# Attention and routed experts on one core: queries and keys transposed by DMA instead of TensorE and ScalarE

## The chip, the core and the metric

The kernel runs on one NeuronCore of a Trainium2 chip. The metric is the device time of one execution in microseconds (us). TensorE is PE in the profile, VectorE is DVE, ScalarE is ACT, GpSimd is POOL and SyncE is SP. Two queues carry nearly all DMAs: q1, whose DMAs SP issues, and q0, whose DMAs POOL issues.

## The reference

```python
# x: (2, 2048, 256); 4 heads of 64; 8 experts
x = x + ln(attention(ln(x)))
x = x + ln(moe(ln(x)))

def attention(x):
    xn = layernorm(x, ln_gamma, ln_beta)
    q, k, v = heads(xn @ w_q.T), heads(xn @ w_k.T), heads(xn @ w_v.T)
    qn = q / max(norm(q) * 64 ** -0.5, 1e-8) * q_gamma * 64 ** -0.5
    kn = k / max(norm(k) * 64 ** -0.5, 1e-8) * k_gamma
    return softmax(qn @ kn.T) @ v @ w_o.T + b_o          # heads put together again

def moe(x):
    e = argmax(x @ gate_w.T)
    return x + expert_w[e] @ x
```

Inputs and outputs are float32.

## The kernel before

The two batches are worked one after the other. For each there is a projection stage, a score stage and an output stage; the experts come behind both. In the projection stage 2048 tokens are taken as 16 tiles of 128 (`n` counts tiles over both batches, `t` is the tile in its group of four). TensorE projects a tile into two alternating PSUM banks (`ps_QK[t % 2]`, and another pair for the values). The rest of the tile's work is a line of small instructions, with an order written out by hand on each engine:

- ACT `squares` (L595 to L601): squares of queries and keys, the values' high half, and the gate copy. DVE `sums` (L964, L967): sums of the squares, and the values' low half.
- ACT `norms` (L618): the root. DVE `normal_qk` (L972, L975, L983): guard against zero, reciprocal, normalized queries and keys in float32.
- POOL (L459, L463): gamma on the queries, their squares. ACT `high_qk` (L626) and DVE `low_qk` (L992, L995): the float32 values are split into a high and a low float16 part, which lie beside each other in a row buffer `qk_s[t % 2]`, with tokens on partitions and 8 blocks (4 heads of queries, 4 of keys) of 128 columns.
- PE `transpose_qk` (L1461, L1463): eight 128x128 transposes into banks 6 and 7. ACT `move_q` and `move_k` (L632, L637) copy them into `q_T` and `k_T`; DVE's `move_q` (L1092) does the last two tiles' queries.
- SP `turned_keys` (L334, L335): after each group of four tiles, two DMAs copy the group's keys into the other plane of `k_T` with the 64-row halves swapped.

`high_qk` of tile n waits until the transposes of tile n-2 have read the same row buffer. On TensorE the order is projection of tile n+1, then transposes of tile n-1; the projection of n+1 waits for `normal_qk` of n-1, whose bank it takes. On ACT `high_qk` of n-1 stands between `squares` and `norms` of n.

Before the projection of batch 0, SP has put three large transfers on q1: the fill of `rows_d` (L324, 5,180 KB) and two of expert weights (L329, 512 KB each). Batch 1's stage has DVE's `page` work (routing) behind its first tile, and POOL issues one scatter for each tile (L434).

In the score stage, for each of 128 steps of a batch (4 heads, 2 blocks of 1024 queries, 16 tiles of keys), TensorE makes 128x1024 scores, ACT the exponentials (L695), a cast DMA that POOL issues (L482) the high half, DVE the low half (L1128), and TensorE 24 products with the values (L1618, L1619, L1620). The row buffers `qk_s` lie in the memory of the exponentials' float16 slots 2 and 3, so the first steps of the score stage wait for the last transposes. Group gi's keys are awaited before step 4 gi through `s_kc`.

## Time and profile before

| | us |
|---|---|
| median of 3 runs | 696.52 (695.33 to 700.66) |
| the profiled execution | 696.07 |
| its span in the trace | 694.3 |
| TensorE busy | 607.2 (87%) |
| VectorE busy | 579.8 (84%) |
| ScalarE busy | 536.5 (77%) |
| GpSimd busy | 262.9 (38%) |

By the timeline the projection stages run from about 25 to 82 us and from 312 to 382 us, the score stages from there to 275 and 570 us, and the rest is the output stages and the experts. A busy share is an average over these stages, which have different limits, so each stage is read by itself.

### The profile page before, as it was taken

What the parts mean: (1) busy time and instruction counts of PE and PEld (TensorE: products, weight loads), DVE (VectorE), ACT (ScalarE), POOL (GpSimd) and SP (SyncE); (2) the same over time, 40 slices, a digit from 0 to 9 for tenths busy, and PEclk for the clock granted to TensorE, in tenths of its full rate; (3) what the DMA queues carried; (4) which work ended last, traced back from release to release, by engine and by line L of the source; (5) the groups of instructions that cost most, each with busy time, mean ns of one, the idle gap of its engine ahead of it and who ended that gap; (6) DMA issues with size and microseconds to landing.
All of it is one profiled execution on the core that took longest, in us unless ns stands there. A gap on an engine that the chain in (4) does not pass through costs nothing.

```text
span 694.3 us, 21582 instructions
## 1 busy us (share of the span) xinstructions
PE 607.2 (87%) x8717; PEld 424.6 (61%) x8717; DVE 579.8 (84%) x1147; ACT 536.5 (77%) x876; POOL 262.9 (38%) x430
## 2 busy tenths in 40 slices
PE   4889789999999999877998899999999998658871
PEld 2667446666656667745766366666666677536761
DVE  5999868998898899898999588888988888977663
ACT  4688879888988899765897878888888897445552
POOL 4344433333333332002677433333323320455554
PEclk9999989999999999999999999999999999979997
DMA  5951198989889997122122888988898974119211
GB/s 165 290 130 31 33 182 163 171 156 184 166 157 168 170 172 149 64 62 68 47 85 69 159 155 156 165 156 162 155 166 151 165 135 124 55 69 314 72 58 47
DMA packets 60665, 92.88 MB, mean 134 GB/s; under 512 B 7057, under 2 KB 29844, under 8 KB 60566
## 3 DMA queue, kind: packets, MB, share of 16 engines
q0 software_dynamic: 35088, 66.13, 49.6%
q1 hardware_dynamic: 24902, 25.37, 12.8%
q8 instruction: 69, 1.13, 0.7%
q14 instruction: 30, 0.25, 0.1%
q10 hardware_dynamic: 576, 0.00, 0.0%
HBM read 15.87 MB, written 14.66 MB: 44 GB/s over the span
## 4 chain that ended last, share of the span: by engine, by line
PE 50%; DVE 25%; ACT 9%; issue 7%; DMA 5%; POOL 1%; another core or an unknown queue 1%; SPq 0%; POOLq 0%; DVEq 0%; ACTq 0%
PE banks L1576 18%; PE banks L1619 7%; PE banks L1618 7%; PE banks L1620 7%; PE banks L1370 5%; DVE e_l L1128 4%; DMA e_h<-e_f 2%; ACT e_f L695 2%; DVE x_all L1201 2%; PE banks L1420 2%; DMA e_x<-x_all 2%; ACT x_all L695 2%; DVE st L1214 1%; DVE e_l L983 1%; PE banks L1468 1%
## 5 line engine op out<-in xcount | busy, mean ns | idle before, releaser
L695 ACT ACTIVATE e_f<-banks,nbias,c_ 128x1024 f32<-128x1024 f32 x172 | 200.6, 1202 | 43.2 <-PE banks L1576 31.4
L1576 PE MATMUL banks<-q_T,k_T 128*128 128x512 f16 (+1 forms) x1024 | 217.2, 384 | 9.1 <-DVE e_l L983 3.9
L1620 PE MATMUL banks<-v_mm,e_l 128*128 128x65 f16 x2048 | 203.4, 192 | 0.0
L1620 PEld LDWEIGHTS banks<-v_mm,e_l 128*128 128x128 f16 x2048 | 187.9, 98 | 0.0
L1128 DVE TENSOR_TENSOR e_l<-e_f,e_h 128x1024 f16<-128x1024 f32 x100 | 120.1, 1224 | 20.4 <-DMA e_h<-e_f 13.5
L1618 PE MATMUL banks<-v_mm,e_h 128*128 128x65 f16 x1184 | 118.9, 193 | 1.2 <-issue 0.6
L1619 PE MATMUL banks<-v_mm,e_h 128*128 128x64 f16 x1184 | 119.1, 194 | 0.0
L1618 PEld LDWEIGHTS banks<-v_mm,e_h 128*128 128x128 f16 x1184 | 108.9, 97 | 13.6 <-issue 2.2
L1619 PEld LDWEIGHTS banks<-v_mm,e_h 128*128 128x128 f16 x1184 | 108.5, 97 | 9.8
L1576 PEld LDWEIGHTS banks<-q_T,k_T 128*128 128x128 f16 (+1 forms) x1024 | 51.3, 96 | 99.6 <-issue 62.1
L695 ACT ACTIVATE x_all<-banks,nbias,c_ 128x1024 f32<-128x1024 f32 x84 | 98.9, 1201 | 6.9 <-DVE e_l L1128 5.5
L1128 DVE TENSOR_TENSOR e_l<-e_f,e_x 128x1024 f16<-128x1024 f32 x72 | 86.5, 1223 | 10.5 <-DMA e_x<-e_f 6.2
L1619 PE MATMUL banks<-v_mm,e_x 128*128 128x64 f16 x864 | 87.2, 194 | 0.0
L1618 PE MATMUL banks<-v_mm,e_x 128*128 128x65 f16 x864 | 87.2, 193 | 0.0
L1618 PEld LDWEIGHTS banks<-v_mm,e_x 128*128 128x128 f16 x864 | 79.4, 97 | 11.3 <-issue 4.0
L482 POOL DMA_DIRECT2D e_h<-e_f x86 | 46.1, 536 | 101.9 <-PE banks L1620 66.0
L1619 PEld LDWEIGHTS banks<-v_mm,e_x 128*128 128x128 f16 x864 | 79.2, 97 | 6.9
L482 POOL DMA_DIRECT2D e_x<-e_f x62 | 33.1, 534 | 80.9 <-PE banks L1620 62.4
L1128 DVE TENSOR_TENSOR e_l<-x_all,e_h 128x1024 f16<-128x1024 f32 x48 | 57.9, 1225 | 2.2 <-DMA e_h<-x_all 1.4
L459 POOL TENSOR_TENSOR e_l<-e_l,gq 128x256 f32<-128x256 f32 x32 | 33.8, 1055 | 67.2 <-DVE e_l L983 66.8
L1128 DVE TENSOR_TENSOR e_l<-x_all,e_x 128x1024 f16<-128x1024 f32 x36 | 43.7, 1221 | 6.2 <-DMA e_x<-x_all 6.0
L434 POOL DMA_INDIRECT rows_d<-attn_x,rowat x32 | 32.1, 1002 | 31.1 <-DVE rowat L1295 18.6
(304 smaller groups left out, 1257.1 us busy)
## 6 DMA issues: line engine op xcount, KB each, us to landing
e_h<-e_f POOLq DMA_DIRECT2D x86, 256.0 KB, 3.8
e_x<-e_f POOLq DMA_DIRECT2D x62, 256.0 KB, 3.7
e_h<-x_all POOLq DMA_DIRECT2D x42, 256.0 KB, 4.1
e_x<-x_all POOLq DMA_DIRECT2D x30, 256.0 KB, 4.6
x_all<-x SPq DMA_DIRECT2D x12, 512.0 KB, 4.2
rows_d<-e_x SPq DMA_DIRECT2D x1, 5180.0 KB, 25.5
k_T<-k_T SPq DMA_DIRECT2D x16, 256.0 KB, 3.6
k_T<-rows_d SPq DMA_DIRECT2D x15, 259.0 KB, 5.5
```

What stands on the lines that cost most here:

```text
L434: pool.indirect_dma_start(out=rows_d, out_offset=bass.IndirectOffsetOnAxis(ap=rowat[:, b * NT + i:b * NT + i + 1], axis=0), in_=x1_all[:, ...
L459: pool.tensor_tensor(qv, qv, spread(gq[:, :], 1, H), ALU.mult).then_inc(s_qg, 1)
L482: pool.dma_start(high[s % ALL % NHI], whole[s % ALL % NEF]).then_inc(s_cast[s % ALL % NHI], 16)
L695: act.activation(whole[s % ALL % NEF], ps_S[s % ALL % 3], ACT.Exp, bias=bias_of(h, k // NT), scale=CESC).then_inc(s_E, 1)
L1128: dve.tensor_tensor(low[s % ALL % NLO], whole[s % ALL % NEF], high[s % ALL % NHI], ALU.subtract).then_inc(s_El, 1)
L1201: dve.scalar_tensor_tensor(out=x_all[:, 2 * i + t, :], in0=ps_Y[i][t][:, 0:D], scalar=rs1[:, i % 2, t:t + 1], in1=x_all[:, 2 * i + t, :], ...
L1370: ins = pe.matmul(dst, l, r, start=(i == 0), stop=(i == n - 1))
L1420: pe.matmul(ps_QK[t % 2], l, r, start=i == 0, stop=False)
L1576: return pe.matmul(ps_S[s % ALL % 3][:, c * BANK:(c + 1) * BANK], k_T[rows, 1 - c if cross else c, h * N + j * P:h * N + (j + 1) * P], q_T ...
L1618: pe.matmul(o, high[s % ALL % NHI][:, at], v[:, 0:DH + 1], start=first, stop=False, skip_group_check=True)
L1619: pe.matmul(o[:, 0:DH], high[s % ALL % NHI][:, at], v[:, VL:VS], start=False, stop=False, skip_group_check=True)
L1620: ins = pe.matmul(o, low[s % ALL % NLO][:, at], v[:, 0:DH + 1], start=False, stop=j == NT - 1, skip_group_check=True)
```

## The change

Three edits. First, the eight transposes and two copies of a tile are replaced by two transposing DMAs on SP's queue, one for the queries (128x512 float16 in, four blocks of 128x128 out) and one for the keys. They count on `s_tr[n % 2]`, 32 a tile. What waited for the transposes (`high_qk`, POOL's and DVE's first steps of the score stage, TensorE's first scores, the keys' swap) now waits for these DMAs to land. Second, the guard of the norm (L972) is merged into the multiplication that follows: `min(1/norm, limit) * value` is one scalar_tensor_tensor, and the scale of the keys moves into constants. Third, the values' low halves leave the buffer `v_mm`, where they began at a byte that isn't a multiple of 8 in half of the cases, and get a tile `v_lo` of their own; the rows of `v_mm` become 68 elements long.

```diff
-        v_mm = sb("v_mm", [P, NT * H, VS], f16)       # VS = 130
+        v_mm = sb("v_mm", [P, NT * H, VS], f16)       # VS = 68
+        v_lo = sb("v_lo", [P, NT * H, DH], f16)
...
+            def transposed_qk(n, at):
+                sp.wait_ge(s_lo, n + 1)
+                if n == 0:
+                    sp.wait_ge(s_wf, 2)
+                for i, plane in ((0, 0), (1, 1 + swapped(at))):
+                    sp.dma_start_transpose(qk_T[:, plane, :].rearrange("p (h n) -> p h n", h=H)[:, :, at * P:(at + 1) * P],
+                                           qk_rows[n % 2][:, i * H * P:(i + 1) * H * P]).then_inc(s_tr[n % 2], 16)
+
+            def turned_keys(b, gi):
+                a = swapped(gi * TG)
+                for i in range(2):
+                    sp.wait_ge(s_tr[i], transposed(b * NT + (gi + 1) * TG - 2 + i))
...
+            def queries_and_keys(b):
+                for at in range(NT):
+                    transposed_qk(b * NT + at, at)
+                    if at % TG == 0 and at:
+                        turned_keys(b, at // TG - 1)
+                turned_keys(b, NG - 1)
...
                     if s == b * ALL + 2:
-                        pool.wait_ge(s_T2, b * NT + NT - 1)
+                        pool.wait_ge(s_tr[0], transposed(b * NT + NT - 2))
...
                 def high_qk(n, t):
...
                     if n - 1 > 0:
-                        act.wait_ge(s_T2, n - 1)
+                        act.wait_ge(s_tr[t % 2], transposed(n - 2))
...
-                        if not (first and t < 2):
-                            move_k(n - 2, at - 2)
-                            move_q(n - 2, at - 2)
...
                         if h == 0 and k == 0:
                             high_qk(end - 1, NT - 1)
-                            move_k(end - 2, NT - 2)
-                        if h == 0 and k == 1:
-                            move_k(end - 1, NT - 1)
...
-                    dve.scalar_tensor_tensor(out=nm[:, :], in0=nr[:, :], scalar=RMS_EPS, in1=rcol[:, :],
-                                             op0=ALU.max, op1=ALU.mult).then_inc(s_dq, 1)
-                    dve.wait_ge(s_dq, 2 * n + 1)
-                    dve.reciprocal(rn[:, :], nm[:, :]).then_inc(s_dq, 1)
+                    dve.reciprocal(rn[:, :], nr[:, :]).then_inc(s_dq, 1)
...
-                    dve.tensor_tensor(qk_n[t % 2].rearrange("p (h d) -> p h d", d=DH),
-                                      ps_QK[t % 2].rearrange("p (h d) -> p h d", d=DH),
-                                      spread(rn[:, :], 2, DH), ALU.mult).then_inc(s_qkn, 1)
+                    dve.scalar_tensor_tensor(out=qk_n[t % 2].rearrange("p (h d) -> p h d", d=DH), in0=spread(rn[:, :], 2, DH),
+                                             scalar=KSCALE / RMS_EPS, in1=ps_QK[t % 2].rearrange("p (h d) -> p h d", d=DH),
+                                             op0=ALU.min, op1=ALU.mult).then_inc(s_qkn, 1)
...
                     if s == b * ALL + 2:
-                        dve.wait_ge(s_T2, end)
+                        dve.wait_ge(s_tr[1], transposed(end - 1))
...
-                        if not (first and t < 1) and not (last and t == TG - 1):
-                            transpose_qk(n - 1, t - 1)
...
-                        pe.matmul(o[:, 0:DH], high[s % ALL % NHI][:, at], v[:, VL:VS], start=False, stop=False, skip_group_check=True)
+                        pe.matmul(o[:, 0:DH], high[s % ALL % NHI][:, at], v_l, start=False, stop=False, skip_group_check=True)
```

## Rows read from the trace of the kernel before

**Rows 1.** The page's first line: the span.
```profile
span 694.3 us, 21582 instructions
```

**Rows 2.** Busy times by stretch: PE, PEld, DVE, ACT, POOL, granted clock, DMA share, GB/s.
```profile
322.65:333.36 10.71, 8.18 (x45) 5.54 (x43) 10.26 (x35) 4.02 (x10) 5.57 (x6) 0.84 0.07 25
333.36:349.00 15.64, 13.63 (x99) 10.68 (x97) 14.11 (x40) 13.91 (x35) 9.76 (x11) 1.00 0.24 69
349.00:363.30 14.30, 13.27 (x96) 10.60 (x96) 13.07 (x31) 13.29 (x33) 10.48 (x13) 1.00 0.25 72
363.30:377.70 14.40, 13.33 (x94) 10.19 (x92) 13.00 (x32) 11.31 (x30) 10.35 (x12) 1.00 0.25 74
```

**Rows 3.** Timeline of two tiles: start us, us, engine, line, operation, idle before it.
```profile
366.68 0.68 DVE L992 TENSOR_TENSOR e_h<-e_l,e_h 128x512 f16<-128x512 f32 x1
...
368.21 0.69 DVE L964 TENSOR_REDUCE ss<-e_f 128x8 f32<-128x512 f32 x1 [0.41 <-ACT e_f L595]
...
369.35 0.17 DVE L972 SCALAR_TENSOR_TENSOR nm<-nr,rcol 128x8 f32<-128x8 f32 x1
...
371.14 0.40 PE L1461 MATMUL banks<-ident,e_l 128*128 128x128 f16 x4 [0.46 <-DVE e_l L992]
...
371.57 0.71 PE L1420 MATMUL banks<-wqkv_h,n_h 128*128 128x512 f32 x2
...
371.70 0.63 ACT L626 ACTIVATE e_h<-e_l 128x512 f16<-128x512 f32 x1
```

**Rows 4.** Groups by line and shape, 349.0 to 377.7 us: busy, mean ns, idle before.
```profile
L964 DVE TENSOR_REDUCE ss<-e_f 128x8 f32<-128x512 f32 x8 | 5.4, 681 | 1.7 <-ACT e_f L595 1.7
L972 DVE SCALAR_TENSOR_TENSOR nm<-nr,rcol 128x8 f32<-128x8 f32 x8 | 1.3, 164 | 0.3
...
L632 ACT ACTIVATE q_T<-banks 128x512 f16<-128x512 f16 x8 | 4.9, 614 | 0.0
L637 ACT ACTIVATE k_T<-banks 128x512 f16<-128x512 f16 x8 | 4.8, 603 | 0.0
```

**Rows 5.** The swap of the keys, the two issuing lines L334 and L335.
```profile
L334 SPq DMA_DIRECT2D k_T<-k_T x8: 590/591/716, 44.4 to 387.4; - x8
...
DMA to landing us min/median/max: 3.2/3.3/3.4
...
L335 SPq DMA_DIRECT2D k_T<-k_T x8: 608/624/640, 45.2 to 388.0; - x8
...
DMA to landing us min/median/max: 3.7/4.1/4.4
```

**Rows 6.** The page's table of queues: packets, MB, share of 16 engines' span.
```profile
q1 hardware_dynamic: 24902, 25.37, 12.8%
```

**Rows 7.** Start of batch 0: weights' issues, landing, DMA share, ACT.
```profile
L329 SPq DMA_DIRECT2D x_all<-weT x2: 483/4776/9070, 21.3 to 30.4; - x2
...
DMA to landing us min/median/max: 12.8/16.6/20.4
...
42.00:44.00 2.00, 1.39 (x12) 1.26 (x13) 2.00 (x5) 2.00 (x7) 1.72 (x2) 1.00 0.08 33
...
35.52 0.64 ACT L626 ACTIVATE e_h<-e_l 128x512 f16<-128x512 f32 x1
```

**Rows 8.** Timeline where batch 1's projection ends and its scores begin.
```profile
386.73 0.60 ACT L637 ACTIVATE k_T<-banks 128x512 f16<-128x512 f16 x1 [0.70 <-PE banks L1463]
...
387.23 2.30 ACT L695 ACTIVATE e_f<-banks,nbias,c_ 128x1024 f32<-128x1024 f32 x2
...
389.27 0.53 POOL L482 DMA_DIRECT2D e_h<-e_f  x1 [2.38 <-ACT e_f L695]
```

**Rows 9.** Timeline of the products with the values, head 0 and head 3.
```profile
390.24 0.19 PE L1618 MATMUL banks<-v_mm,e_h 128*128 128x65 f16 x1 [0.30 <-issue]
...
390.87 0.19 PE L1618 MATMUL banks<-v_mm,e_h 128*128 128x65 f16 x1
...
540.31 0.19 PE L1618 MATMUL banks<-v_mm,e_h 128*128 128x65 f16 x1
...
540.93 0.19 PE L1618 MATMUL banks<-v_mm,e_h 128*128 128x65 f16 x1
```

More of the change, by code:

```diff
@@ L227, in build @@
         s_kc = [sem(f"s_kc{i}") for i in range(NG)]
+        s_tr = [sem(f"s_tr{i}") for i in range(2)]
         s_id, s_ones, s_wf, s_qg, s_q2 = sems("id ones wf qg q2")
@@ L379, in _ @@
             pool.memset(ones16[:, :], 1.0).then_inc(s_ones, 1)
-            for i in range(2 * H):
-                pool.memset(rcol[:, i:i + 1], 1.0 if i < H else 1.0 / KSCALE).then_inc(s_ones, 1)
             pool.memset(v_mm[:, :, DH:DH + 1], 1.0).then_inc(s_ones, 1)
@@ L1449, in project_first_two @@
                 bias_v(1)
-            def transpose_qk(n, t):
-                qs = qk_s[t % 2]
-                pe.wait_ge(s_lo, n + 1)
-                if (sum(pb < b for pb, _, _ in PASSES) - 1) * PAGE + 2 > 0:
-                    pe.wait_ge(s_pg, (sum(pb < b for pb, _, _ in PASSES) - 1) * PAGE + 2)
-                if n > 0:
-                    pe.wait_ge(s_qe, n)
-                if n > 0:
-                    pe.wait_ge(s_ke, n)
-                for h in range(H):
-                    pe.transpose(ps_TQ[:, h * P:(h + 1) * P], qs[:, h, :], ident16[:, :])
-                for h in range(H):
-                    ins = pe.transpose(ps_TK[:, h * P:(h + 1) * P], qs[:, H + h, :], ident16[:, :])
-                ins.then_inc(s_T2, 1)
             def keep_running(count):
@@ L1609, in pv @@
                     pe.wait_ge(s_El, s + 1)
-                    v = v_mm[:, j * H + h, :]
+                    v, v_l = v_mm[:, j * H + h, :], v_lo[:, j * H + h, :]
                     for q in range(QT):
@@ L1657, in _ @@
                 hh = b * H
-                pe.wait_ge(s_ke, end - 3)
-                pe.wait_ge(s_qe, end - 3)
+                pe.wait_ge(s_tr[0], transposed(b * NT + QT - 2))
+                pe.wait_ge(s_tr[1], transposed(b * NT + QT - 1))
                 pe.wait_ge(s_mx, b + 1)
@@ L1663, in _ @@
                 scores(hh, 0, 1)
-                transpose_qk(end - 2, NT - 2)
                 pe.wait_ge(s_vl, end)
@@ L1673, in _ @@
                 largest_everywhere(1)
-                pe.wait_ge(s_ke, end)
                 pe.wait_ge(s_root, 9 * b + 1)
```

70 lines of the change are left out of this document (22 added, 48 removed).

## The prediction

> **What bounds the kernel now.** I read the page first: a span of 694.3 us [rows 1] in an execution of 696.07 us, so 1.8 us lie around the span, and the execution is 0.45 us under the median of the runs (696.52). My sum is made against 696.07. The busy shares cover stages with different limits, so I went on to the busy times by stretch. In the score stages TensorE sets the pace, and the change touches only the operands of its products with the values. In the projection stages three engines are nearly full at once: over tiles 8 to 15 of batch 1 (28.7 us, 3.59 us a tile) PE, DVE and ACT are busy 26.6, 26.1 and 24.6 us [rows 2]. The four tiles before, which also carry DVE's statistics for a later group, take 3.91 us each with DVE busy 14.11 of 15.64 us. So no engine is alone the bound, and the chain alternates between them. The groups by line say what DVE waits for: 1.7 of its 2.6 idle us are for ACT's squares [rows 4], which wait for a projection, which waits behind the transposes, which wait for `low_qk` (0.46 us in [rows 3]). That is the ring which the change cuts.
>
> **What is taken away.** Per tile, PE loses 8 transposes, 0.43 us from the first to the next projection (371.14 to 371.57, [rows 3]). ACT loses two copies, 0.61 + 0.60 us [rows 4]. DVE loses L972, 0.16 us, with the gap to the next about 0.21. PE's and ACT's savings count only as far as they shorten DVE's waits. So with free transposes tiles 8 to 15 lose 1.7 us of waits and 8 x 0.21 = 1.7: 28.7 becomes 25.3, or 3.16 us a tile, and DVE is then the bound. Tiles 4 to 7 lose 4 x 0.21 = 0.8. In batch 1 the projection behind the page work no longer waits for the first transposes: 0.6. At the end of the stage ACT no longer waits 0.70 us for the last transposes and copies them before the third exponential (386.73, then 387.23, [rows 8]), and an earlier copy goes too: 1.5. Together 3.4 + 0.8 + 1.5 = 5.7 us in batch 0 and 6.3 in batch 1, 12.0 in all. That is the most that the change can give.
>
> **Edits I cost at nothing.** L983 becomes a scalar_tensor_tensor over the same 512 float32 elements; no row has that form at that size. Bounds are 0 and 0.05 us a tile (1.6 us in all); I take 0. The values' alignment: the rows of `v_mm` are 260 bytes apart, so with the head number both halves pass through every offset of 4 bytes in 16. Head 0 makes 21 products from 390.24 to 390.87 and head 3 makes 21 from 540.31 to 540.93 [rows 9]: 0.63 and 0.62 us, one pace at opposite alignments. Nothing is gained there.
>
> **What is added: two DMAs a tile, with a round trip in a ring.** `high_qk` of tile n now waits until both DMAs of tile n-2 have landed. Call D the time from the end of `low_qk` to that landing. In the trace L992 ends at 367.36 and `high_qk` of the tile two further starts at 371.70 [rows 3]: 4.34 us, while two tiles last 7.1. `norms`, behind it on ACT, could come about 0.3 us later before DVE misses it. So D may be 2p - 2.5 at a pace of p a tile, or p = (D + 2.5) / 2. A late `high_qk` holds `norms`, then `normal_qk`, then the next projection: everything. At 3.59 us a tile D may be 4.7 us; for the best pace of 3.16 it must be under 3.8.
>
> What is D? The trace has no transposing DMA. The nearest row is the swap of the keys on the same queue [rows 5]: 0.59 us to issue, 3.2 to 3.4 us from issue to landing for the first and 3.7 to 4.4 for the second right behind it. It moves 256 KB in 256 pieces of 1 KB. If a transposing DMA costs no more, D = 0.1 + 0.59 + 3.3 to 4.1 = 4.0 to 4.8, the lower bound in practice. But a transposing DMA has no pieces of 1 KB: each row of the input holds four blocks of 128 columns, 256 bytes each, that go to different places, so it has at least 128 x 4 = 512 pieces. The queue's row gives 16 x 694.3 us x 0.128 / 24,902 = 57 ns a packet of about 1 KB on one engine [rows 6]. The swap's 16 pieces an engine take 0.9 of its 3.3 us, which leaves 2.4 that are fixed. The transposing DMA's 32 pieces an engine take 1.8 us at the price of a packet and 0.5 at the price of the bytes. The upper bound is pieces of a quarter of that size at the same price, 7.3 us a DMA. I take the price of a packet with pieces of 256 bytes, the middle case and the one nearest to the row: D = 0.1 + 2.4 + 2 x 1.8 = 6.1 us, p = 4.3.
>
> Then tiles 8 to 15 cost (4.33 - 3.59) x 8 = 5.9 us more, tiles 4 to 7 (4.33 - 3.91) x 4 = 1.7, the two before them about 0.8, and the swaps of the keys, which now stand between transposes on SP (2 x 0.6 us of issue) and put 0.9 us of packets each ahead of them, about 0.5 in each of three groups, 1.5. That is 9.9 us a batch, 19.8. The end of the stage still gains, but the third cast now waits for tile 14's DMAs instead of ACT, so I count 1.0 of the 1.5 in each batch: -2.0; and -0.6 behind the page work. The keys' last group is needed only at step 12, and hidden.
>
> The Trainium skill (VectorE: DVE Perf Modes, "The three transpose paths") puts a 128x128 transpose of 2-byte elements at 1309 ns by DMA against 390 ns on TensorE. No row here shows it; it speaks against the change. Taken one after the other, eight blocks would be an estimated 10.5 us a tile, and the whole near 890 us.
>
> **A stall at the start of batch 0.** SP's queue is not empty there. The second weights' issue starts at 30.4 us and lands 12.8 us later, at 43.2, and the DMA share falls to 0.08 only from 42 on [rows 7]. Tile 0's transposes are issued at about 31.3, behind those bytes, and can't land before them. `high_qk` of tile 2 ran at 35.52 [rows 7] and would wait to 43.2: 7.7 us, with DVE, ACT and PE all behind it. The bounds are 0, if the transposes pass the weights, and about 9, if TensorE's clock drops in the pause as it did to 0.84 around a similar one [rows 2].
>
> Sum: 19.8 - 2.0 - 0.6 + 7.7 = +24.9, and 696.1 + 24.9 = 721.
>
> **The rivals.**
> - *The round trip fits.* D = 4.3, p = 3.4. Tiles 8 to 15 gain 1.5 a batch, with 0.8 and 1.5 as above: 3.8 a batch and 0.6, 8.2 in all, against the stall of 7.7: 695.6, about no change. For it: the swap of the keys lands in 3.3 us with twice the bytes. Against: its pieces are four times larger. Chance 0.33, from 690 to 699. The Trainium skill (Advanced Engine Details and Errata, "X-Bar Transpose (TRN2)") says that transposing DMAs are as fast as regular ones; that is this rival, and by the page its 695.6 us would be the time.
> - *Faster.* The transposes are not held behind the weights at 31 us, and D is under 3.8, so DVE bounds at 3.16 us a tile: 696.1 - 12.0 = 684. It decides at one place, the stall: without its 7.7 us even the case above gives 688. Against: one queue, and 9.07 us for an issue in front of it that found the queue full [rows 7]. Chance 0.09.
> - *Much slower.* The pieces are 64 bytes or cost more than a packet: 7.3 us a DMA and 14.6 a tile, and the pace is that of the engines. 28 tiles x (14.6 - 3.7) = +305, about 1000 us at the bound; anything over 770 belongs here. Chance 0.13.
> - *The transposes don't matter*, because POOL's scatters and gamma (10.4 of 14.3 us busy in batch 1, [rows 2]) take over as the bound: then batch 1 gains nothing and batch 0's gain pays half of its stall, about 700. It is inside the first rival's sign and I give it 0.03.
>
> **How the numbers follow.** The forecast case has 0.42, from 703 (D = 5) to 770 (D = 8.5 to 9, or SP's issue twice as long). Together with the case that fits, the range is 690 to 770; under it lies 0.09 and over it 0.13. The likeliest case's own range is 703 to 770. About 1% is what a measurement of this kernel can tell from no change. Faster by over 1% (under 689.5) has 0.09, within 1% 0.36, slower 0.55. The predicted time is 721 us.
>
> **What would show it.** The landing of the two new DMAs on SP: I expect 5.5 to 6.5 us from `low_qk` to the second landing, and about 12 us for the first tile of batch 0, behind the weights. ACT's `high_qk` should show idle time ended by a DMA in most tiles; if its releaser is POOL as before, D fits. The starts of L964 should be 4.3 us apart in tiles 8 to 15; 3.2 to 3.4 would say that the ring fits, over 6 that the DMA engines or SP's issue bound. The issue of a transposing DMA should take 0.6 to 0.8 us; if it takes 2, SP is the bound and the forecast is low. Between 35 and 43 us all three engines should pause. L1618 should keep 30 ns from one product to the next. The prediction falls if the new DMAs land within 4 us, if tile 2 doesn't wait for the weights, or if packets of the new DMAs cost other than 57 ns.

## The result

| | median us | runs | ratio to before |
|---|---|---|---|
| before | 698.55 | 4 | |
| after | 708.23 (707.02 to 711.74) | 4 | 1.0166, 95% interval 1.0127 to 1.0205 |

The changed kernel is slower by 1.7%. (The kernel before has one run more here, 700.57 us, than the three behind the median of 696.52.) The profiled execution took 707.02 us, with a span of 705.3 us against 694.3 [rows 1]: +11.0 us, where the forecast had +24.9. The direction was right; the size was more than twice too large.

The page of the kernel after: the span, the engines' busy time, the granted clock in 40 slices, SP's queue (packets, MB, share of 16 engines' span) and the chain that ended last.

```profile
span 705.3 us, 20987 instructions
...
PE 601.7 (85%) x8461; PEld 416.7 (59%) x8461; DVE 572.2 (81%) x1111; ACT 509.1 (72%) x816; POOL 261.0 (37%) x422
...
PEclk9959979999999999999999899999999999879996
...
q1 hardware_dynamic: 59718, 33.77, 19.4%
...
PE 49%; DVE 23%; DMA 8%; issue 6%; ACT 6%; SPq 5%; POOL 1%; POOLq 0%; another core or an unknown queue 0%; ACTq 0%; DVEq 0%
```

SP's queue carries 59,718 packets instead of 24,902 [rows 6]. The 64 transposing DMAs account for the 34,816 more, 544 each. The line of the chain now has 8% of DMA and 5% of SP's queue, where the kernel before had 5% and 0%. The busy times by stretch (PE, PEld, DVE, ACT, POOL, granted clock, DMA share, GB/s) follow. The stretches are those of [rows 2], each moved by 11.02 us, because batch 1's tile 0 starts that much later:

```profile
333.67:344.38 10.71, 6.77 (x37) 4.31 (x36) 10.28 (x33) 4.15 (x12) 5.95 (x7) 1.00 0.25 61
344.38:360.02 15.64, 12.74 (x64) 9.64 (x62) 13.43 (x33) 10.09 (x26) 10.19 (x12) 0.89 0.41 99
360.02:374.32 14.30, 11.37 (x64) 8.85 (x64) 11.99 (x28) 10.17 (x25) 10.27 (x12) 1.00 0.64 150
374.32:388.72 14.40, 12.97 (x61) 9.55 (x61) 11.11 (x26) 6.79 (x19) 9.81 (x11) 0.88 0.67 122
```

In the third stretch PE and ACT are emptier than before (11.4 and 10.2 us against 13.3 and 13.3), and DVE, which was to become the bound, waits too (12.0 against 13.1). In the fourth DVE has 11.1 us against 13.0, and the granted clock, 1.00 before, is 0.88.

**Where the time went.** The last product of each tile's projection (the bias of the values, L1418; L1432 before) marks the tiles. These are its rows in the timeline of TensorE for tiles 0, 4, 5 and 15 of batch 0 and tiles 0 and 15 of batch 1, by start and duration:

```profile
19.84 0.28 PE L1418 MATMUL banks<-bq,ones 128*128 128x264 bf16 x1
...
36.44 0.44 PE L1418 MATMUL banks<-bq,ones 128*128 128x264 bf16 x1
...
49.92 0.44 PE L1418 MATMUL banks<-bq,ones 128*128 128x264 bf16 x1
...
88.18 0.29 PE L1418 MATMUL banks<-bq,ones 128*128 128x264 bf16 x1
...
325.99 0.29 PE L1418 MATMUL banks<-bq,ones 128*128 128x264 bf16 x1
...
388.18 0.29 PE L1418 MATMUL banks<-bq,ones 128*128 128x264 bf16 x1
```

From such rows, and for the last two columns from the last product of the scores, the stages of every kernel follow. All later uses of "stages" mean this table (us, in profiled executions; the labels are those of the experiments below):

| kernel | to tile 0 | projection, batch 0 | scores and output, batch 0 | projection, batch 1 | scores, batch 1 | rest | span |
|---|---|---|---|---|---|---|---|
| before | 20.9 | 57.6 | 236.5 | 62.5 | 191.5 | 125.4 | 694.3 |
| after | 19.8 | 68.3 | 237.8 | 62.2 | 192.1 | 125.0 | 705.3 |
| e1 merge only | 20.8 | 55.0 | 235.3 | 60.8 | 190.9 | 125.7 | 688.4 |
| e10 the same again | 21.6 | 55.0 | 235.5 | 59.8 | 190.4 | 125.6 | 687.8 |
| e2 clear start | 21.3 | 64.0 | 237.4 | 63.3 | 194.0 | 126.9 | 706.9 |
| e3 plain copies | 21.6 | 65.3 | 235.2 | 60.6 | 190.4 | 123.8 | 696.9 |
| e4 one DMA | 20.8 | 69.1 | 238.5 | 61.4 | 192.5 | 127.6 | 709.9 |
| e11 boundary order | 20.8 | 66.6 | 238.1 | 64.1 | 192.1 | 129.4 | 711.2 |
| e12 third DMA | 21.5 | 74.8 | 243.6 | 72.1 | 201.3 | 129.2 | 742.5 |
| e9 queries from tile 5 | 21.6 | 54.5 | 237.0 | 59.8 | 191.4 | 126.4 | 690.7 |
| e5 late fill * | 20.4 | 59.4 | 248.2 | 62.1 | 192.9 | 114.9 | 697.9 |
| e6 fillers * | 21.8 | 65.4 | 236.2 | 63.6 | 193.9 | 115.3 | 696.1 |
| e7 queries by DMA * | 21.5 | 65.1 | 234.6 | 59.0 | 192.0 | 114.5 | 686.8 |
| e8 merge, late fill * | 21.7 | 55.0 | 244.5 | 59.7 | 191.2 | 113.6 | 685.6 |

The four kernels with a star ran on another chip, where the last stage is 10 to 12 us shorter and the kernel before took 685.98 us. They are read by their other stages and by ratios to before on that chip.

The first two rows hold the result: +10.7 us in batch 0's projection, +1.3 behind it, and nothing else that counts. Batch 1's projection, for which the forecast had +9.3 (9.9 - 0.6; its gain of 1.0 at the end of the stage lies behind tile 15 and so in the next column), came out 0.3 us shorter. 13.5 us of batch 0 lie between two tiles, 36.44 to 49.92. ACT shows why. These are its rows for `high_qk` (L640) of tile 2, and of tile 9 in batch 1, with the idle time before and its releaser:

```profile
43.68 0.63 ACT L640 ACTIVATE e_h<-e_l 128x512 f16<-128x512 f32 x1 [11.63 <-DMA qk_T<-e_h]
...
371.40 0.63 ACT L640 ACTIVATE e_l<-e_l 128x512 f16<-128x512 f32 x1 [1.10 <-DMA qk_T<-e_l]
```

and SP's timeline around both (start, duration of the issue, count of instructions that the row merges):

```profile
31.49 7.13 SPq L336 DMA_TRANSPOSE qk_T<-e_h  x2
38.66 3.78 SPq L336 DMA_TRANSPOSE qk_T<-e_l  x2
...
366.97 2.50 SPq L336 DMA_TRANSPOSE qk_T<-e_l  x2
369.91 2.50 SPq L336 DMA_TRANSPOSE qk_T<-e_h  x2
372.51 0.60 SPq L343 DMA_DIRECT2D qk_T<-qk_T  x1
373.15 0.62 SPq L344 DMA_DIRECT2D qk_T<-qk_T  x1
373.82 3.15 SPq L336 DMA_TRANSPOSE qk_T<-e_l  x2
```

Tile 0's transposes are issued at 31.49 and release ACT at 43.68, 12.2 us later, where the prediction had "about 12". In the steady state a pair is issued in 2.50 us and has released ACT 4.4 us after the issue began (366.97 to 371.40). That is the first surprise: over half of the 4.4 us is the issue. All 64 together, the source view of L336 (min/median/max of the issue in ns):

```profile
L336 SPq DMA_TRANSPOSE qk_T<-e_h x32: 1188/1267/3837, 31.5 to 394.8; - x32
L336 SPq DMA_TRANSPOSE qk_T<-e_l x32: 1188/1268/2417, 38.7 to 398.4; - x32
```

The 1.3 us behind batch 0's projection go with a wait for DMAs too. The row buffers lie in memory that the first steps of the score stage need, so DVE's low half of the third step waits for the transposes of the last tile:

```profile
106.22 1.23 DVE L1114 TENSOR_TENSOR e_l<-e_f,e_h 128x1024 f16<-128x1024 f32 x1 [3.67 <-DMA qk_T<-e_l]
```

It starts 18.0 us behind tile 15's last product, where the kernel before had 15.6, and the sixth low half 24.5 us behind it, where the kernel before had 23.4.

**The last group boundary.** By the same rows the distances inside the groups of batch 1 are 3.2 us a tile for tiles 8 to 11 (362.75 to 372.23 in three steps) and 3.0 for tiles 12 to 15, against 3.6 and 3.4 before: the 3.16 of "free transposes" is there between the boundaries. But tile 12 stands 7.0 us behind tile 11 (4.0 before). TensorE's row there:

```profile
375.21 0.83 PE L1406 MATMUL banks<-wqkv_h,n_h 128*128 128x512 f32 x2 [2.69 <-DVE n_l L956]
```

and the stretches around it:

```profile
368.00:372.00 4.00, 4.00 (x29) 3.43 (x28) 3.06 (x7) 2.04 (x7) 3.56 (x5) 1.00 0.59 132
372.00:375.00 3.00, 0.51 (x5) 0.27 (x3) 2.80 (x5) 2.37 (x7) 2.06 (x3) 1.00 0.72 168
375.00:379.50 4.50, 4.29 (x15) 3.30 (x16) 2.98 (x8) 0.53 (x2) 3.21 (x4) 0.62 1.10 163
```

ACT waits 1.10 us for the transposes of tile 7, the tile two ahead in the same row buffer (371.40 above). Behind that on ACT stand the root of the norms and the high half of the next group's rows, and behind those on DVE stands their low half `n_l` (L956). TensorE idles 2.69 us for it, and for the next 4.5 us its granted clock is 0.62, near the lower of its two levels (1.2 of 2.4 GHz).

### The profile page after: what moved, and what is told of

It reads as the page before. It is cut to its first block, busy times and chain, and to the rows that moved or that the text cites. A ratio compares the mean times of both kernels' runs of the same rounds, so it can differ in the third digit from the quotient of the medians.

```text
span 705.3 us, 20987 instructions
## 1 busy us (share of the span) xinstructions
PE 601.7 (85%) x8461; PEld 416.7 (59%) x8461; DVE 572.2 (81%) x1111; ACT 509.1 (72%) x816; POOL 261.0 (37%) x422
## 3 DMA queue, kind: packets, MB, share of 16 engines
q1 hardware_dynamic: 59718, 33.77, 19.4%
## 4 chain that ended last, share of the span: by engine, by line
PE 49%; DVE 23%; DMA 8%; issue 6%; ACT 6%; SPq 5%; POOL 1%; POOLq 0%; another core or an unknown queue 0%; ACTq 0%; DVEq 0%
PE banks L1543 19%; PE banks L1585 7%; PE banks L1587 7%; PE banks L1586 7%; DMA qk_T<-e_l 4%; DVE e_l L1114 4%; SPq L336 4%; PE banks L1356 3%; ACT e_f L694 2%; DVE x_all L1187 2%; PE banks L1406 2%; DVE st L1200 2%; DVE e_l L976 1%; DMA qk_T<-e_h 1%; ACT x_all L694 1%
## 5 line engine op out<-in xcount | busy, mean ns | idle before, releaser
L1543 PE MATMUL banks<-qk_T 128*128 128x512 f16 (+1 forms) x1024 | 220.8, 388 | 12.3 <-DVE e_l L976 7.6
L1114 DVE TENSOR_TENSOR e_l<-e_f,e_h 128x1024 f16<-128x1024 f32 x100 | 120.8, 1226 | 22.4 <-DMA e_h<-e_f 10.7
L1585 PE MATMUL banks<-v_mm,e_h 128*128 128x65 f16 x1184 | 119.0, 195 | 3.9 <-DVE e_l L1114 2.8
L1586 PE MATMUL banks<-v_lo,e_h 128*128 128x64 f16 x1184 | 119.0, 193 | 0.0
L1585 PEld LDWEIGHTS banks<-v_mm,e_h 128*128 128x128 f16 x1184 | 108.6, 98 | 16.4 <-DVE e_l L1114 3.9
L1543 PEld LDWEIGHTS banks<-qk_T 128*128 128x128 f16 (+1 forms) x1024 | 51.8, 97 | 107.3 <-issue 66.7
L1586 PEld LDWEIGHTS banks<-v_lo,e_h 128*128 128x128 f16 x1184 | 108.1, 99 | 9.7
L1585 PE MATMUL banks<-v_mm,e_x 128*128 128x65 f16 x864 | 86.4, 194 | 0.0
L1586 PE MATMUL banks<-v_lo,e_x 128*128 128x64 f16 x864 | 86.3, 192 | 0.0
L1585 PEld LDWEIGHTS banks<-v_mm,e_x 128*128 128x128 f16 x864 | 78.7, 97 | 11.3 <-issue 2.5
L1586 PEld LDWEIGHTS banks<-v_lo,e_x 128*128 128x128 f16 x864 | 78.4, 98 | 6.9
L496 POOL DMA_DIRECT2D e_x<-e_f x62 | 33.1, 534 | 86.1 <-PE banks L1587 63.3
L448 POOL DMA_INDIRECT rows_d<-attn_x,rowat x32 | 32.0, 1000 | 31.6 <-DVE rowat L1281 20.8
## 6 DMA issues: line engine op xcount, KB each, us to landing
rows_d<-e_x SPq DMA_DIRECT2D x1, 5180.0 KB, 24.9
```

Source lines behind the costliest of these rows:

```text
L448: pool.indirect_dma_start(out=rows_d, out_offset=bass.IndirectOffsetOnAxis(ap=rowat[:, b * NT + i:b * NT + i + 1], axis=0), in_=x1_all[:, ...
L496: pool.dma_start(high[s % ALL % NHI], whole[s % ALL % NEF]).then_inc(s_cast[s % ALL % NHI], 16)
L1114: dve.tensor_tensor(low[s % ALL % NLO], whole[s % ALL % NEF], high[s % ALL % NHI], ALU.subtract).then_inc(s_El, 1)
L1543: return pe.matmul(ps_S[s % ALL % 3][:, c * BANK:(c + 1) * BANK], k_T[rows, 1 - c if cross else c, h * N + j * P:h * N + (j + 1) * P], q_T ...
L1585: pe.matmul(o, high[s % ALL % NHI][:, at], v[:, 0:DH + 1], start=first, stop=False, skip_group_check=True)
L1586: pe.matmul(o[:, 0:DH], high[s % ALL % NHI][:, at], v_l, start=False, stop=False, skip_group_check=True)
```

## The experiments

My theory after the result had three parts: the merged guard is a gain of its own; the ring of DMAs costs a little in every group; and the start of batch 0 costs a lot once. The rivals: the merge gives nothing, the start is a matter of the queue's order, and the boundary's idle time and clock are what costs. The edits are shown shortened.

**e1: the merge and the alignment alone.** The change without its DMAs; transposes stay on TensorE.

```diff
-  nr = sqrt(ss / DH);  nm = max(nr, eps) * rcol;  rn = 1 / nm;  qk_n = ps_QK * rn
+  nr = sqrt(ss / (DH * KSCALE**2));  rn = 1 / nr;  qk_n = min(rn, KSCALE / RMS_EPS) * ps_QK
+  v_lo = sb("v_lo", [P, NT * H, DH], f16)
```

> The kernel before with only the merged norm guard and the values' low halves in a tile of their own; the transposes stay on TensorE. If both edits matter only by the instruction they take from VectorE, each of 32 tiles loses about 0.2 us of which a part is hidden: 2 to 5 us faster than before (ratio 0.993 to 0.997), and the products with the values keep 30 ns. The rival, that the alignment of the low halves sets the pace of the products, would give 0.5 ns or more on each of 6144 products, 3 us on top, and a shorter spacing of L1618's successor.

Measured: 690.51 us against 697.04, ratio 0.9919 (0.9890 to 0.9949). Stages: batch 0's projection 55.0 us (57.6 before), batch 1's 60.8 (62.5), the others within 1.2 us of before. So the two small edits give 4.3 us in the projections, and 6.5 us in the whole, a little over the 2 to 5 expected. It is the guard: DVE's low half of the values takes 473 ns in both kernels, aligned or not. Set against this kernel, the DMAs cost 13.3 us in batch 0's projection and 1.4 to 2.4 in batch 1's.

**e10: the same again, on a third chip**, beside e9, e11 and e12.

> The kernel before with the merged guard and the aligned low halves alone, transposes on TensorE, once more and on the same chip as the other three, so that they can be set against it: 0.992 of before again (0.989 to 0.995 the first time), if the ratios carry over from chip to chip.

Measured: 694.30 against 698.83, ratio 0.9932 (0.9907 to 0.9957). The gain is real and carries over. The profiled execution was the fastest of six (689.49 us), so its span, 687.8, flatters this kernel.

**e2: a clear start.** The changed kernel with the fill of `rows_d` on POOL's queue, and the experts' first weights issued behind tile 8.

```diff
-  sp.dma_start(rows_d..., absent...)                       # before the transposes
+  pool.dma_start(rows_d..., absent...)
-  for k in range(KH): sp.dma_start(raw_we[:, k], ...)      # before the transposes
+  if b == 0 and at == 8: for k in range(KH): sp.dma_start(raw_we[:, k], ...)
```

> The changed kernel, with the 5,180 KB fill issued on GpSimd's queue and the first expert weights issued behind the transposes of tile 8, so that SP's queue is empty when the first transposes are issued. If the changed kernel loses its time at that one place (ScalarE's wait of 11.6 us for the first transposes of the row buffer e_h), it becomes 8 to 11 us faster than the changed kernel: 697 to 700 us, no change against before. If the round trip of every tile sets the pace, the wait moves to the later tiles and less than 3 us come back: 705 or more.

Measured: 710.37, ratio 1.0222 (1.0176 to 1.0269). ACT's row for tile 2, the stretches of the start, and the source view of the fill:

```profile
40.65 0.63 ACT L642 ACTIVATE e_h<-e_l 128x512 f16<-128x512 f32 x1 [7.18 <-DMA qk_T<-e_h]
```

```profile
18.00:28.00 10.00, 9.95 (x66) 8.05 (x65) 9.32 (x28) 6.76 (x21) 4.04 (x7) 1.00 1.04 302
28.00:38.00 10.00, 6.52 (x28) 4.77 (x27) 7.54 (x21) 3.95 (x10) 2.33 (x3) 0.76 1.07 258
```

```profile
L423 POOL DMA_DIRECT2D rows_d<-e_x x1: 2233/2233/2233, 14.3 to 14.3; - x1
...
DMA to landing us min/median/max: 25.4/25.4/25.4
```

Nothing stands ahead of the transposes on SP's queue any more, and ACT still waits 7.2 us. What is left is the fill on the other queue, issued at 14.3 us and landed at 39.7, with the DMA share over 1 from 18 to 38 us (1.04, 1.07). The trace has the single DMA packets too: the first one of the transposes starts at 35.36, 5.1 us behind the issue at 30.23, where it is 1.2 us in the steady state. So the order of one queue explains only part of the wait; transfers of the other queue hold the transposes back too. The prediction had blamed the weights in front of them on SP. Batch 0's projection is 4.3 us shorter than in the changed kernel, but the kernel isn't: the other stages are about 6 us longer together. DVE's waits for the last tiles' transposes (5.9 us against 3.7) are a part of that; for the rest I have no cause.

**e5 and e8: the fill behind batch 0's scores.** e5 is the changed kernel, e8 that of e1. In both POOL issues the fill when the score stage of batch 0 ends; in e5 the weights are behind tile 8 as well.

```diff
+  if b == 0:
+      pool.wait_ge(s_PV, ALL)
+      pool.memset(absent, NTOK);  pool.dma_start(rows_d..., absent...)
```

> The changed kernel with the 5,180 KB fill moved behind batch 0's score stage (issued by GpSimd, from the same memory) and the first weights behind tile 8's transposes. In the run that only changed the queue of the fill, ScalarE still waited 7.2 us for the first transposes, with the DMA engines at a share of 1.0 to 1.1 until 39.7 us, when the fill landed. Theory: the DMA engines, not the queue, hold the first transposes. Then, with the engines free, ScalarE's first wait for a DMA in batch 0 falls under 1 us, tile 15's projection starts 7 to 9 us sooner than in the changed kernel (79 to 81 us instead of 88), and the time becomes 699 to 703 us, unless the fill gives 1 to 3 us back in the output stage. Rival: the first transposing DMAs are slow by themselves (the first issue in the trace took 3.8 us); then a wait over 4 us stays, and the time stays over 705.

> The kernel before with the merged guard, the values' own tile and the late fill, all transposes on TensorE. It is the control of the late fill alone: in batch 0's projection stage nothing waits for a DMA, so the late fill should give nothing there, and at most 2 us either way in the output stage: 689 to 693 us against 690.5. If it is 3 us or more faster, the fill held something in the first 40 us in the kernel before too, and that part of the gain of the changed kernel with the late fill is not the transposes'.

Measured: e5 699.43 against 685.98, ratio 1.0208 (1.0185 to 1.0230); e8 686.81, ratio 1.0006 (0.9991 to 1.0020). e5's row for tile 2:

```profile
33.45 0.63 ACT L645 ACTIVATE e_h<-e_l 128x512 f16<-128x512 f32 x1 [0.86 <-DMA qk_T<-e_h]
```

The wait falls from 11.63 to 0.86 us and batch 0's projection from 68.3 to 59.4: the stall of the start is the DMA engines' load, and it is worth 8.9 us. (The two kernels ran on different chips; e1 and e8, on the same two, both have 55.0 us in this stage.) But the fill costs 10.4 us where it now stands (248.2 against 237.8), and 9.2 in e8 (244.5 against 235.3), so moving it wins nothing. The two kernels also give the price of the DMA way with no stall at the start. e5's projections are 4.4 and 2.4 us longer than e8's, and its span is 12.3 us longer. Of the other 5.4 us of stages, 3.7 lie in the scores and output of batch 0, 1.7 in batch 1's scores and 1.3 in the rest, less 1.3 before tile 0. In both score stages DVE's third low half waits for the last tile's transposes, 4.11 and 2.70 us, and the sixth comes 1.6 and 0.8 us later than in e8; for the remainder I have no cause.

**e3: plain copies.** The two transposing DMAs are replaced by plain copies of the same bytes from and to the same places. Queries and keys are then not transposed, and the factor of the exponent is set to 0, so this kernel leaves out the transposition and its scores mean nothing; tokens may be routed otherwise, and its last stage isn't compared.

```diff
-  sp.dma_start_transpose(qk_T[:, plane]..., qk_rows[n % 2][...])
+  sp.dma_start(qk_T[:, plane]..., qk_rows[n % 2][...].rearrange("p (h n) -> p h n", h=H))
-  dve.tensor_scalar(CESC, tmp[3], 1.0 / (KSCALE * sqrt(DH)), ...)
+  dve.tensor_scalar(CESC, tmp[3], 0.0, ...)
```

> The changed kernel with each transposing DMA replaced by a plain DMA over the same bytes and blocks (so queries and keys aren't transposed; the factor of the exponent is set to zero to keep the numbers finite). It prices the transposing itself. If a transposing DMA costs more than a copy by its issue on SP (1.2 us against about 0.6) and its landing, the copies land about 1.3 us sooner, ScalarE's waits for DMAs fall from 25 us to under 10 us outside the first tile, and the time falls by 2 to 5 us. If the landing is set by the number of 256-byte pieces, the same for both, the time stays within 1 us of the changed kernel.

Measured: 700.39 against 697.04, ratio 1.0054 (1.0028 to 1.0079). The source view of the copies:

```profile
L336 SPq DMA_DIRECT2D qk_T<-e_h x32: 593/641/3052, 32.8 to 388.1; - x32
L336 SPq DMA_DIRECT2D qk_T<-e_l x32: 594/641/4221, 36.7 to 390.7; - x32
...
  ACT e_h L640: 11.9, 1
  ACT e_l L640: 1.9, 2
```

A copy's issue takes 0.64 us, half a transposing DMA's. With it ACT waits for these DMAs three times in all instead of 15: once 11.9 us at the start, where copies are held back like transposes, and 1.9 us in two others. Batch 1's projection is 60.6 us, as with the merge alone. So away from the start a pair of copies is hidden, and what the ring notices is what a pair of transposing DMAs costs beyond it. That is the issue, 2.50 us a pair instead of 1.28. By the DMA packets in the two traces, a pair in batch 1 that nothing disturbs has its last packet 3.9 us behind the start of its issue as transposes and 2.6 us as copies, but 1.4 us behind the end of its issue as either.

**e4: one DMA of eight blocks** in place of two of four, in the two groups where queries and keys lie side by side.

```diff
-  for i, plane in ((0, 0), (1, 1)): sp.dma_start_transpose(qk_T[:, plane]..., ...)
+  sp.dma_start_transpose(qk_T[:, 0:2]..., qk_rows[n % 2])      # 128x1024 in, 8 blocks out
```

> The changed kernel with one transposing DMA of eight blocks instead of two of four in the first and third group of each batch, two as before in the second and fourth. If the issue of a transposing DMA costs by the block (a piece at a time from SP), the single one takes about 2.4 us on SP, as the two together do, and nothing changes. If it costs by the instruction, it takes about 1.25 us, the pair of groups shows a landing 1.2 us sooner, and 2 to 4 us are gained.

Measured: 711.65 us, one execution. SP's timeline, where L337 is the pair of four-block DMAs and L340 the single one of eight blocks:

```profile
370.37 2.50 SPq L337 DMA_TRANSPOSE qk_T<-e_l  x2
373.41 1.23 SPq L340 DMA_TRANSPOSE qk_T<-e_h  x1
```

Eight blocks are issued in 1.23 us, like four: the issue goes by the instruction. Yet the projections are no shorter (69.1 and 61.4 us against 68.3 and 62.2). By the packets the single DMA is done 2.6 us behind the start of its issue, where the pair takes 3.9: the round trip is shorter by the issue that is saved. Yet halving the issue in half of the groups didn't show in the whole, in this one execution.

**e6: fillers at the boundary.** Eight products without use ahead of TensorE's wait at each boundary.

```diff
   if t == TG - 1:
+      if g: keep_running(8)
       pe.wait_ge(s_ys, g + 2)
```

> The changed kernel with 8 products that nobody reads (about 1.8 us) on TensorE before the first projection of each group but the second. In the changed kernel TensorE is idle for 2.7 us there and the projection then runs at the granted clock of 1.2 GHz: 4.0 us instead of 2.6. Theory: the transposes on TensorE also kept its clock up, and their removal costs about 1.4 us at each boundary. Then with the products the projections behind the boundaries take 2.6 us again, and 3 to 6 us come back (702 to 705 us). Rival: the pace is that of the DMAs' round trip and the slow projections are hidden by it: the time stays within 1.5 us of the changed kernel's.

Measured: 698.59 against 685.98, ratio 1.0196 (1.0179 to 1.0213). TensorE's row at the boundary and the stretch from it:

```profile
374.46 0.73 PE L1406 MATMUL banks<-wqkv_h,n_h 128*128 128x512 f32 x2 [2.61 <-DVE n_l L956]
```

```profile
374.00:377.00 3.00, 2.54 (x9) 1.76 (x10) 2.97 (x7) 0.40 (x2) 1.92 (x3) 0.76 0.81 177
```

The fillers were done at 371.85, and TensorE still idled 2.61 us; the clock still fell, and over the 4.5 us from the restart it is 0.62, as in the changed kernel (375.21 to 379.71). The experiment doesn't separate idle time from clock, and is inconclusive on that; e11 does.

**e7: queries alone by DMA,** keys on TensorE and ScalarE, with the merge.

```diff
-  for h in range(H): pe.transpose(ps_TQ[:, h * P:(h + 1) * P], qs[:, h, :], ident16)   # and move_q on ACT
+  sp.dma_start_transpose(q_T[...][:, :, at * P:(at + 1) * P], qk_rows[n % 2][:, 0:H * P])
```

> The kernel before with the merged guard and the values' own tile, and only the queries transposed by DMA (one a tile); the keys stay on TensorE and ScalarE. By the theory that the round trip of two DMAs (2.5 us of issue and about 2 us to land) is what costs, one of them costs half of the issue, 1.25 us, and lands 3.2 us after the low half is written, inside the 4.3 us that the ring leaves; only the start of batch 0 still waits for the fill. So it lies between: 4 to 8 us slower than the 690.5 us of the same kernel without DMAs (694 to 699). If the number of DMAs doesn't matter and the boundaries and the start cost the same, it is as slow as the changed kernel, 706 or more.

Measured: 689.71 against 685.98, ratio 1.0063 (1.0044 to 1.0083). ACT's row for tile 2:

```profile
44.76 0.63 ACT L643 ACTIVATE e_h<-e_l 128x512 f16<-128x512 f32 x1 [10.11 <-DMA q_T<-e_h]
```

Half of the DMAs leave the start as bad as all (65.1 us for batch 0's projection). Batch 1's is 59.0 us, 0.7 under e8's on the same chip. Away from the start, one transposing DMA a tile is hidden; two are not. The ratio of 1.0063 is above what had been expected (at most 699 us, 1.003), because the stall at the start stayed whole.

**e9: queries by DMA from tile 5 of batch 0 on.** As e7, but tiles 0 to 4 take the old way, so that nothing is transposed by DMA while the fill and the weights are under way.

```diff
+  FD = 5
+  if b * NT + at >= FD: transposed_q(b * NT + at, at)     # on SP
-  move_q(n - 2, at - 2)
+  if n - 2 < FD: move_q(n - 2, at - 2)                    # on ACT
```

> The kernel before with the merged guard and the aligned low halves; keys stay on TensorE and ScalarE, and queries go by one transposing DMA a tile, but only from tile 5 of batch 0 on: tiles 0 to 4 take the old way, so nothing waits for a transposing DMA while the fill of the rows and the weights hold the DMA engines. Theory A (the loss of the DMA way is the start of batch 0 and the wait at the last group boundary, both of which this leaves out; elsewhere one DMA a tile that is issued in 1.25 us and has landed within about 4.4 us is hidden): batch 0's projection about 54 us (55.0 with the merge alone), batch 1's about 59 to 60 (60.8), ScalarE's casts of the high halves wait for no DMA, and the kernel is 1 to 2 us below the merge alone: ratio to before about 0.990. Theory B (each transposing DMA costs time wherever it stands, as SP's queue, the keys' swap or the shared write port is held by it): batch 0's projection 56 us or more, ratio 0.995 or more, above the merge alone.

Measured: 692.65 against 698.83, ratio 0.9919 (0.9893 to 0.9946), beside e10's 694.30 and 0.9932. Batch 0's projection takes 54.5 us, and ACT's waits in both projections name no DMA: the start is avoided as theory A had it. Batch 1's is 59.8, no shorter than e10's. The two versions can't be told apart: the intervals overlap, and by spans e9 is the longer (690.7 against 687.8), but e10's is that of its fastest execution. Both are faster than the two kernels of this case.

**e11: another order at the boundary.** In the third tile of a group, ACT takes the norms' root and the next group's high half ahead of `high_qk`, and DVE the low half ahead of `low_qk`.

```diff
+  if t == 2: norms(n);  high_y(g + 1)
   high_qk(n - 1, t - 1)
-  norms(n) ... if t == 2 and not last: high_y(g + 1)
+  if t != 2: norms(n)
```

> The changed kernel with another order in the third tile of each group alone: ScalarE takes the tile's root and the high half of the next group's rows ahead of the cast that waits for the transposing DMA, and VectorE the low half of those rows ahead of the low half of the queries and keys. Theory A (at a boundary the wait for the transposes of two tiles ago, 1.10 us at 371.40, is passed on through this order to the next group's rows, TensorE idles 2.7 us and comes back at half clock): the start distance over the last boundary falls from 7.0 and 8.1 us to about 4.5, the granted clock there stays at full, each batch's projection is 2 to 4 us shorter (about 65 and 59 to 60 us), and the ratio falls from 1.017 to about 1.009. Theory B (the boundary is late for another reason, such as the group's rows themselves or TensorE's clock): distances stay at 7 and 8 us and the ratio at 1.015 to 1.02.

Measured: 712.02 against 698.83, ratio 1.0169 (1.0135 to 1.0203), that of the change itself. TensorE's row at the boundary, then its stretch, then SP and ACT behind it:

```profile
374.19 0.73 PE L1409 MATMUL banks<-wqkv_h,n_h 128*128 128x512 f32 x2 [0.43 <-DVE n_l L959]
```

```profile
374.00:377.00 3.00, 2.81 (x15) 2.10 (x15) 2.97 (x8) 1.67 (x6) 1.61 (x2) 1.00 0.77 185
```

```profile
374.76 2.51 SPq L336 DMA_TRANSPOSE qk_T<-e_l  x2
...
380.97 0.63 ACT L640 ACTIVATE e_l<-e_l 128x512 f16<-128x512 f32 x1 [2.88 <-DMA qk_T<-e_l]
```

This was the most useful experiment. At the boundary everything happened as theory A said: TensorE idles 0.43 us instead of 2.69, the granted clock stays at 1.00, and tile 12 starts 3.2 us behind tile 11 (7.0 in the kernel after; 3.5 for 8.1 in batch 0). And nothing was gained, where that theory had about 0.8%: 2.88 us of waiting appear in the next round, for the transposes that were issued at 374.76, just behind the swap of the keys. The wait at the boundary was where the ring's debt was paid, not its cause. It also takes the clock out of the account: at 1.00 instead of 0.62 the kernel was no faster.

**e12: a third transposing DMA a tile,** the keys once more into the half that the swap overwrites.

```diff
-  for i, plane in ((0, 0), (1, 1 + swapped(at))):
+  for i, plane in ((0, 0), (1, 1 + swapped(at)), (1, 2 - swapped(at))):
```

> The changed kernel with a third transposing DMA a tile: the keys once more, into the half that the swap of the keys overwrites later, so that the results are the same. Theory A (the time of a transposing DMA is its issue, 1.25 us on SP, and its packets, 544 of about 22 ns each: the third adds at least 1.25 us to the time D from low halves to landed, and the two-buffer ring gives a pace of (D + 2.5)/2, but SP needs 3.75 us a tile and so sets it): the pace inside the groups of batch 1 rises from 3.2 us to 3.8 to 4.2, batch 1's projection from 62 us to 70 to 76, batch 0's by as much, and the ratio is 1.04 to 1.06. Theory B (the ring has room, what costs is only the start and the boundary): pace stays at 3.2 to 3.4 us, ratio below 1.03.

Measured: 742.42 against 698.83, ratio 1.0634 (1.0584 to 1.0683), a little over theory A's range. The source view:

```profile
L336 SPq DMA_TRANSPOSE qk_T<-e_h x48: 1188/1267/4602, 31.5 to 422.9; - x48
```

The issue of one stays at 1.27 us. Batch 0's projection is 74.8 us (+6.5) and batch 1's 72.1 (+9.9). In batch 1 tiles 8 to 12 take 19.5 us, 4.9 a tile, against 16.5 with two DMAs. Twelve issues of 1.27 and two of the swap make 16.5 us of SP's time a group, so SP isn't alone the bound; the ring is. The score stages grew as well, by 5.8 and 9.2 us. The last tiles' transposes are still being issued when they begin (until 430.4 in batch 1, tile 15's last product starting at 412.0), and DVE waits for them:

```profile
438.29 2.36 DVE L1114 TENSOR_TENSOR e_l<-e_f,e_h 128x1024 f16<-128x1024 f32 x2 [9.32 <-DMA qk_T<-e_l]
```

In batch 0 that wait is 3.90 us. The sixth low half comes 5.3 and 10.2 us later behind tile 15 than in the changed kernel, which accounts for the growth to within 1 us.

## Why the prediction was right in direction and wrong in size

**"The most that the change can give", 12.0 us.** Part of it needs no DMAs: by the medians e1 is 6.5 us shorter than before on its chip and e10 4.5. The prediction counted only 0.21 us a tile for the merged guard, 5.0 us over the 24 tiles that it named, or 6.7 over all 32; measured are 2.6 and 1.7 us in the two projections of e1, and 2.6 and 2.7 in e10. So the size is about right. More was never seen: e9, the best use of the DMAs here, can't be told apart from the guard alone.

**Edits at nothing.** Held. L976 takes 0.687 us a tile, where L983 took 0.691 over the whole run: the scalar_tensor_tensor costs what the tensor_tensor did. The products with the values keep their pace: in head 3, L1585 starts at 547.84, 547.93 and 548.02, one of three products each 0.03 us, with both halves aligned.

**D, the round trip: the step that failed.** The forecast put D at 6.1 us, as 0.1 + 2.4 fixed + 2 x 1.8 for packets at 57 ns, with an issue of 0.6 to 0.8 us. Measured is about 4.5 us: in the steady state `low_qk` ends at 366.94, and the pair issued at 366.97 releases ACT at 371.40. The cast and the low half of that tile are:

```profile
364.65 0.63 ACT L640 ACTIVATE e_l<-e_l 128x512 f16<-128x512 f32 x1 [0.45 <-DMA qk_T<-e_l]
...
366.25 0.69 DVE L985 TENSOR_TENSOR e_l<-e_l 128x512 f16<-128x512 f32 x1
```

Both terms were off, in opposite ways. The packets were counted nearly right, 544 a DMA against "at least 512", but at the wrong price. The queue's busy share rose from 12.8% of 694.3 to 19.4% of 705.3 us, 48 us for each of 16 engines, and 48 x 16 / 34,816 makes 22 ns a packet; in e12 the third DMA's cost 27 ns. A packet of 256 bytes isn't priced like one of 1 KB. That takes 2 x 1.1 us off the sum. The issue was mis-sized the other way: 1.25 us each, 2.5 a pair. The sum had the second issue at nothing, hidden behind 1.8 us of the first one's packets. Those take about 0.8 us, so the issues follow one another and set the time instead. The remaining 2 us, from the end of the issue at 369.47 to ACT's release at 371.40, are the second DMA's own flight. By the prediction's own sign, packets that cost other than 57 ns, its mechanism falls.

**p = (D + 2.5) / 2.** The form held. Where no swap is in the way, ACT's two casts into one buffer that end at a DMA start at 364.65 and 371.40 in the kernel after, 6.75 us for two tiles, 3.4 a tile: D = 4.5 and 2.3 us from the cast's start to the end of `low_qk`. (The 3.0 to 3.2 us inside the groups leave out the boundaries, where the difference is made up.) But the swap of the keys always meets the same one of the two buffers. In e11 the pair issued at 374.76 released ACT at 380.97, D = 6.2. That buffer's two turns in a group of four would cost 4.5 + 6.2 + 2 x 2.5 = 15.7 us, or 15.3 with 2.3 for the 2.5; this is an estimate from those rows. Measured for tiles 4 to 8 and 8 to 12 of batch 1: 16.0 and 15.7 us in e11, 15.1 and 16.5 in the kernel after. Before they were 16.2 and 14.7, with the merge alone 15.6 and 14.3 (e1) or 15.1 and 14.3 (e10). So the kernel after takes about 3.95 us a tile, against 3.9 before and 3.7 with the merge alone. That the swap makes up the difference between 3.4 and 3.95 is argued from these rows. No run took the swap off SP's queue or added a third row buffer, which would test it. The forecast had 4.33 and 0.5 for the swap, 17.8 a group. Of the 19.8 us that the forecast charged to the ring, nearly nothing is left against the kernel before, since the ring took about what the merge had given. Against the merge alone it costs 4.4 and 2.4 us (e5 against e8).

**The stall at the start, 7.7 us.** Right in place and near in size: 11.63 us of ACT's wait, of which taking the load away gives back 8.9. The end was forecast at 43.2 us and came at 43.68; the wait is longer because ACT reached the cast at 32.05, not at 35.52. The clock's share that was named as the upper bound is there: the tiles' last products take 0.44 instead of 0.29 us on both sides of the pause. The mechanism was half right. The bytes ahead of the transposes did hold them, but e2 shows that bytes on the other queue do it too, and with no weights ahead the wait still lasts to 40.65. So the closeness of the 7.7 is partly luck.

**The sum.** By stages the +11.0 us of the span are (10.8 as rounded): the stall at the start 8.9 (after against e5); the rest of batch 0's projection 1.8 (e5's 59.4 against 57.6), where the forecast had 9.9; batch 1's projection -0.3, where the forecast had 9.9 - 0.6; +1.3 and +0.6 in the stages behind, where the forecast had -1.0 each; and -0.4 and -1.1 in the rest and ahead of tile 0. The term that failed is the ring's 19.8, for which the two projections show 1.5. The -2.0 at the ends of the stages had the wrong sign as well, a smaller miss: that cast no longer waits for ACT's copies, but the low half behind it waits 3.67 us for the last transposes in batch 0.

**The rivals.** "The round trip fits" was nearer than the forecast on D (4.3 against 4.5 measured) and on p where no swap is in the way (3.4, as measured); it took the time as 695.6 us, with the stall in it. The rule that it leans on, in the Trainium skill (Advanced Engine Details and Errata, "X-Bar Transpose (TRN2)"), that transposing DMAs are as fast as regular ones, holds here for one part and not for the other: behind the end of the issue a pair takes 1.4 us either way, but the issue is 1.27 us against 0.64 in e3. As a whole e3 stands at a ratio of 1.0054 where the change stands at 1.0166. "Faster" needed no stall and D under 3.8; e5 had nearly no stall and remained slower than its control e8 (1.0208 against 1.0006), so the stall alone doesn't decide. "Much slower" is excluded: neither 64-byte pieces nor one block after the other. The price of 1309 ns a block that the Trainium skill gives (VectorE: DVE Perf Modes, "The three transpose paths") would make an estimated 10.5 us for eight blocks; here eight blocks are issued and landed in 4.4 us. "The transposes don't matter" was partly so: in batch 1's projection ACT's waits at L640 are 6.2 us for the DMAs and 3.7 us for POOL's gamma.

## What to carry to other kernels

Before work is moved from an engine to DMAs inside a ring of two buffers, price the issue as well as the flight, and count every other DMA of that queue that falls into the ring: here the swap of the keys, once in four tiles, put the next round trip at 6.2 us instead of 4.5. Look at what the DMA engines are doing at the moment of the first use, on all queues: a transfer that is free in the steady state cost 9 us at the start. Ask also what waits for the last of the moved DMAs when the stage ends. Separate the edits of a bundle: the small merge was worth 0.7 to 0.8%, and the large move hid it.

## What the runs showed of the hardware that I had not expected

- A transposing DMA takes 1.27 us to issue on SP (median of 64), twice a plain copy's 0.64, and an eight-block one no more than a four-block one (1.23). Behind the end of the issue, a pair of transposes and a pair of copies both need 1.4 us to their last packet (kernel after and e3).
- It makes 544 packets for 128x512 two-byte elements, at 22 to 27 ns each by the queue's busy share; the plain copy of e3 makes 528 (58,694 less 24,902, over 64) at about 18.
- After idling 2.69 us TensorE ran at a granted clock of 0.62 for 4.5 us (375 to 379.5); after idling 0.43 us at the same place it ran at 1.00 (e11). Eight products that ended 2.61 us ahead of the restart changed nothing (e6, 0.62).
- The kernel before took 697.04, 685.98 and 698.83 us on three chips. The kernels that were profiled on the fastest one are shorter in the last stage, by 10 to 12 us, and in no other stage by as much.
